# Layer 0 for four pairs at a time, and the first adapter's matrix ahead of it, in a two-layer conditional kernel

## The reference

```
x1[b]  = x[b]  + einsum('ct,cd->dt', x[b], w[subject[b]]) + bias[subject[b]][:, None]
H      = x1[b] @ W.T
xa     = x1[b] @ A[adapter[b]].T                    # rank 16
out[b] = x1[b] + H + (xa @ Bm[adapter[b]].T) * scal[adapter[b]]
```

## Time and profile before

| what | value |
|---|---|
| median of three runs | 266.66 us |
| the profiled execution | 265.84 us |
| its span in the profile | 264.2 us |
| PE busy | 241.5 us, 91% |
| DVE, ACT, POOL busy | 145.2, 113.4, 82.2 us |
| DMA | 36.69 MB, mean 139 GB/s |

### The profile page before, as it was taken

How to read it: one execution, slowest core, us unless ns; L and a number is a source line. 1 busy time by engine, 2 the same in 40 slices (tenths; PEclk the granted TensorE clock), 3 DMA queues, 4 the chain that set the end, 5 groups by cost and what they waited for, 6 DMA issues and landing times.

```text
span 264.2 us, 9940 instructions
## 1 busy us (share of the span) xinstructions
PE 241.5 (91%) x2929; PEld 194.7 (74%) x2930; DVE 145.2 (55%) x244; ACT 113.4 (43%) x189; POOL 82.2 (31%) x284
## 2 busy tenths in 40 slices
PE   0463999899999999999999999999999999999993
PEld 0442888688788888888888887888878887887882
DVE  5657557755565666755575655566675554433200
ACT  2154345544454445444464444544544443333411
POOL 6332342533324333332343332432333333320000
PEclk9977699999999999999999999999999999999999
DMA  6663144555545554655455545555564445552231
GB/s 114 152 186 105 43 133 134 160 139 148 154 144 156 157 159 139 180 154 144 121 177 155 141 140 146 157 152 159 139 188 149 144 127 179 155 156 79 70 78 42
DMA packets 25826, 36.69 MB, mean 139 GB/s; under 512 B 6736, under 2 KB 8784, under 8 KB 25808
## 3 DMA queue, kind: packets, MB, share of 16 engines
q1 hardware_dynamic: 20400, 28.06, 37.2%
q10 hardware_dynamic: 5408, 8.40, 12.3%
HBM read 19.67 MB, written 16.78 MB: 138 GB/s over the span
## 4 chain that ended last, share of the span: by engine, by line
PE 86%; DVE 5%; DMA 3%; issue 2%; ACT 1%; SPq 1%; ACTq 0%; DVEq 0%
PE ps L717 69%; PE ps L702 13%; PE ps L682 2%; DMA x_ring<-in_x_dram 2%; PE ps L664 2%; DVE m_lo L487 1%; DMA ids_i<-in_itok_B_dram 1%; DVE m_f L481 1%; ACT m_hi L563 1%; DVE x L494 0%; ACT x_hi L569 0%; DVE place L453 0%; DVE prec_n L388 0%; PE ps L654 0%; DVE x_lo L502 0%
## 5 line engine op out<-in xcount | busy, mean ns | idle before, releaser
L717 PE MATMUL ps<-m_hi,x_hi 128*128 x264 | 106.9, 405 | 0.8 <-DVE m_lo L487 0.8
L717 PE MATMUL ps<-m_lo,x_hi 128*128 x264 | 103.5, 392 | 0.0
L717 PE MATMUL ps<-m_hi,x_lo 128*128 x264 | 103.4, 392 | 0.0
L502 DVE TENSOR_TENSOR x_lo<-x,x_hi 128x512 fp32r<-128x512 f32 x64 | 44.5, 695 | 86.5 <-ACT x_hi L569 86.5
L359 POOL COPY p_pair<-p_all 64x64 f32 x128 | 45.6, 356 | 135.0 <-DVE x L494 62.0
L578 ACT ACTIVATE o_ring<-ps 128x512 f32<-128x512 f32 x60 | 35.8, 597 | 63.2 <-PE ps L717 62.9
L717 PEld LDWEIGHTS ps<-m_hi,x_hi 128*128 128x128 f32 x264 | 49.9, 189 | 12.6 <-issue 1.6
L717 PEld LDWEIGHTS ps<-m_hi,x_lo 128*128 128x128 f32 x264 | 49.8, 189 | 10.8
L569 ACT ACTIVATE x_hi<-x 128x512 fp32r<-128x512 f32 x64 | 40.4, 632 | 39.8 <-ACT o_ring L578 18.6
L717 PEld LDWEIGHTS ps<-m_lo,x_hi 128*128 128x128 f32 x264 | 49.9, 189 | 9.5
L702 PEld LDWEIGHTS ps<-p_pair,x_ring 64*64 64x64 f32 x2048 | 34.2, 139 | 18.2 <-issue 16.5
(11 more groups left out here) (81 smaller groups left out, 55.5 us busy)
## 6 DMA issues: line engine op xcount, KB each, us to landing
x_ring<-in_x_dram SPq DMA_DIRECT2D x128, 128.0 KB, 2.6
out_dram<-o_ring ACTq DMA_DIRECT2D x64, 128.0 KB, 2.4
out_dram<-o_ring SPq DMA_DIRECT2D x64, 128.0 KB, 2.5
o_ring<-in_L_cond_W_dram SPq DMA_DIRECT2D x4, 256.0 KB, 4.6
a_f<-in_L_cond_A_dram SPq DMA_DIRECT2D x8, 128.0 KB
b_nat<-in_L_cond_Bm_dram SPq DMA_DIRECT2D x1, 256.0 KB, 4.1
p_all<-in_L_cond_weights_dram SPq DMA_DIRECT2D x2, 128.0 KB, 4.3
bias_all<-in_fside_8xS_dram SPq DMA_DIRECT2D x1, 256.0 KB, 5.7
```

The costliest lines, as they stand in the source:

```text
L502: nc.vector.tensor_tensor(x1_lo[:, u % HELD], x1[:, u % 2], x1_hi[:, u % HELD], ALU.subtract).then_inc(x1_lo_ready, 1)
L717: mm = nc.tensor.matmul(ps[:, bank, :], part[:, u % HELD, c, :], m[:, ds(k * (TC * T) + c * T, T)], start=(c == 0 and part is x1_hi and m ...
```

## The change

- Layer 0 is done for four pairs at once, at steps u = 2 and u = 6 alone, for pairs j + 2, j + 4, j + 3, j + 5 in this order; steps u = 0 and u = 4 do none. Step 0 does pairs 2 and 3 as before.
- Two pairs share two banks: an even pair in banks 0 and 1, an odd one in 6 and 7, in columns 0 to 255 or 256 to 511 by u // 2 % 2. The waits on l0_done are counted in the new order, and DVE reads a bank only when both of its pairs are there.
- x is asked for seven pairs ahead instead of six; the ring of x still has four slots.
- The rings p_pair and bias_pair have eight slots instead of four, with POOL's wait counted accordingly.
- Ahead of step 0, PE does the last chunk of W and all four tiles of the first M, and then layer 0 of pairs 0 and 1. DVE and ACT are reordered to match.

```diff
-    AHEAD = 6
+    PR = 8
+    AHEAD = 7
+    L0_QUAD = 4
...
+        def l0_count(j, u):
+            if isinstance(j, int) and j < L0_QUAD:
+                return j + 1
+            return j - u % L0_QUAD + (2, 4)[u % 2]
+
+        def l0_out(u):
+            cols = TC * C * (u // 2 % 2)
+            return ps[:, 6 * (u % 2):6 * (u % 2) + 2, cols:cols + TC * C]
...
             def load_x(j, slot, b):
-                at_least(sp, l0_done, j - XR + 1)
+                at_least(sp, l0_done, j - XR + 1 if isinstance(j, int) and j < XR + L0_QUAD
+                         else j - XR - slot + (1, 3, 2, 4)[slot])
...
-                slot = u % XR
-                at_least(pool, x1_ready, j - XR + 1)
+                slot = u % PR
+                at_least(pool, x1_ready, j - (PR - 1 if n is None else min(PR - 1, HEAD - 1 + (u - HEAD) % BODY)))
...
             def x1_add(j, u):
-                dve.wait_ge(l0_done, j + 1)
+                dve.wait_ge(l0_done, l0_count(j, u))
...
             m_split(0, 0)
+            m_split(1, 1)
+            m_add(2, 2)
+            m_add(3, 3)
             x1_add(0, 0)
-            m_add(2, 2)
+            m_split(2, 2)
             x1_split(0, 0)
-            m_split(1, 1)
-            m_add(3, 3)
-            m_split(2, 2)
+            x1_add(1, 1)
             m_split(3, 3)
-            x1_add(1, 1)
             x1_split(1, 1)
...
-                at_least(pe, x1_ready, j - 1)
+                at_least(pe, x1_ready, j - 1 if isinstance(j, int) and j < L0_QUAD else j - u % L0_QUAD)
...
+            def l0_at(j, u):
+                if isinstance(j, int) and j == 0:
+                    return range(2, L0_QUAD)
+                if u % L0_QUAD == 2 and (not isinstance(j, int) or j + 2 < PAIRS):
+                    return (2, 4, 3, 5)
+                return ()
...
             turn_w(2)
-            layer0_inputs(0, 0)
-            layer0(0, 0)
             turn_w(3)
             m_product(2, 2)
             m_product(3, 3)
             pe.wait_ge(others_ready, 2)
+            layer0_inputs(0, 0)
+            layer0(0, 0)
             layer0_inputs(1, 1)
             layer0(1, 1)
...
             def step(j, u, n):
-                if u % 2 == 0 and (not isinstance(j, int) or j + 2 < PAIRS):
-                    layer0_inputs(j + 2, u + 2)
-                    layer0_inputs(j + 3, u + 3)
+                l0_pairs = l0_at(j, u)
+                for i in l0_pairs:
+                    layer0_inputs(j + i, u + i)
```

More of the change, by code:

```diff
@@ L79, in cond_residual_layers @@
         bias_all = sb("bias_all", [P, S, C])
-        p_pair = sb("p_pair", [P, XR, C])
-        bias_pair = sb("bias_pair", [P, XR, P])
+        p_pair = sb("p_pair", [P, PR, C])
+        bias_pair = sb("bias_pair", [P, PR, P])
         x1 = sb("x1", [P, 2, TC, P])
@@ L489, in x1_add @@
             def x1_add(j, u):
-                dve.wait_ge(l0_done, j + 1)
+                dve.wait_ge(l0_done, l0_count(j, u))
                 at_least(dve, x1_lo_ready, j - 1)
-                bank = l0_banks(u)
                 nc.vector.tensor_tensor(x1[:, u % 2].rearrange("p c (h d) -> p c h d", h=2),
-                                        ps[:, bank:bank + 2, 0:TC * C].rearrange("p h (c d) -> p c h d", c=TC),
-                                        bias_pair[:, u % XR, :].rearrange("p (h d) -> p h d", h=2).unsqueeze(1)
+                                        l0_out(u).rearrange("p h (c d) -> p c h d", c=TC),
+                                        bias_pair[:, u % PR, :].rearrange("p (h d) -> p h d", h=2).unsqueeze(1)
                                         .to_broadcast([P, TC, 2, C]), ALU.add).then_inc(x1_ready, 1)
@@ L618, in _ @@
             act.wait_ge(warmed, 1)
+            m_round(2, 2)
             x1_round(0, 0)
-            m_round(2, 2)
             m_round(3, 3)
@@ L689, in layer0_inputs @@
                 pe.wait_ge(pair_ready, j * 4 + 4)
-                at_least(pe, x1_ready, j - 1)
+                at_least(pe, x1_ready, j - 1 if isinstance(j, int) and j < L0_QUAD else j - u % L0_QUAD)
             def layer0(j, u):
                 slot = u % XR
-                bank = l0_banks(u)
+                x1_t = l0_out(u)
                 for c in range(TC):
@@ L701, in layer0 @@
                             at = c * P + side * C
-                            mm = nc.tensor.matmul(ps[side * C:side * C + C, bank + half, c * C:c * C + C],
-                                                  x_ring[rows, slot, at:at + C], p_pair[rows, slot, :],
+                            mm = nc.tensor.matmul(x1_t[side * C:side * C + C, half, c * C:c * C + C],
+                                                  x_ring[rows, slot, at:at + C], p_pair[rows, u % PR, :],
                                                   start=True, stop=True)
                 mm.then_inc(l0_done, 1)
+            def l0_at(j, u):
[4 more added lines that the diff above has]
+                return ()
             def layer1(j, u, k, bank, done=l1_done, tiles_awaited=False):
@@ L741, in step @@
                 mixed = n_of_mixed(j) is not None
-                if u % 2 == 0 and (not isinstance(j, int) or j + 2 < PAIRS):
-                    layer0_inputs(j + 2, u + 2)
-                    layer0_inputs(j + 3, u + 3)
+                l0_pairs = l0_at(j, u)
+                for i in l0_pairs:
+                    layer0_inputs(j + i, u + i)
                 k = words(pe, regs[:2 if mixed else 1], table[0:1, ds(j * 8 + W_PLACE, 2 if mixed else 1)], K - 1)
-                if u % 2 == 0 and (not isinstance(j, int) or j + 2 < PAIRS):
-                    layer0(j + 2, u + 2)
-                    layer0(j + 3, u + 3)
+                for i in l0_pairs:
+                    layer0(j + i, u + i)
                 if makes_parts(j, u, n) is not None:
```

2 lines of the change are left out of this document (removed).

## The result

The changed kernel takes 277.51 us (median of 4 runs, 276.61 to 278.77) where the kernel before took 266.50 us beside it (4 runs). The ratio is 1.0415, with a 95% interval of 1.0354 to 1.0477: slower, as predicted (278.0 us). The profiled execution took 277.9 us, its span 276.2 us, against 264.2 before. The lines have moved: L711 is layer 0, L734 layer 1, L691 a tile of M, L673 turn_b, L491 m_add, L497 m_split, L503 x1_add, L511 x1_split, L263 the load of x, L256 that of A, L290 SP's store.

What follows compares the result with a forecast made beforehand. PE was taken as the bound (busy 91%, 86% of the chain), other engines as cover. Start 0.1, rounds 9.7 and end 1.65 sum to 11.5; on 265.84 that gives 277.3, with the median 0.82 higher 278.1, said as 278.0; range 269.5 to 281.5.

Steps and rivals of the forecast that it cites:

- batch of four, start to layer 1: PE in the loop: a batch of 128 layer 0 instructions lasts 2.20 us, its second half adding 1.10.
- m_lo holds step 5, restart from the tile: Layer 1 of step 5: PE waits for m_lo and restarts 0.13 us behind it, 4.44 us from the tile of u = 3.
- from there to the batch at u = 2: Loop, u = 6 to u = 2: late x starts the batch at 14.1 us instead of 13.8; price 0.35.
- five rounds: Loop, u = 6 to u = 6: each round +1.95 us, five rounds +9.7.
- end: Last round up to u = 2 (+1.25) and the steps behind it: together +1.65 us.
- start: Ahead of and up to step 2: 2.4 us won but lost waiting for POOL's pair 7; net +0.1 us.
- The batch gone at u = 4: Between tile and layer 1 of step 5: m_lo's chain stays unchanged, so of 1.10 us taken out only 0.2 comes back.
- x at u = 6: Batch at u = 6: SP's late x, behind A, starts it 8.55 us from the tile of u = 3; price 0.7 a round.
- x at u = 2: Batch at u = 2: last x, asked for behind the store of step 7, comes late; price 0.35 us, bounds 0 and 1.0.
- x in time: Rival: x doesn't delay the batch at u = 6, only the m_lo wait remains; +3.4 us, 270.0; chance 0.12.
- PE stays fed: Rival: all 15 changes of kind go (3.0 us) and the start's 2.4 arrive; 261.3 us; chance 0.05.
- The clock: Rival: waits at u = 6 drop the granted clock, 1.7 us lost in each of six rounds; +10, 288; chance 0.06.

Runs made afterwards that it cites:

- q_both: Changed kernel with A asked for at u = 1 instead of u = 3 and the last tile made at u = 2 instead of u = 3: 268.43 us.
- q_a_early: Changed kernel with SP asking for the next adapter's A at u = 1 instead of u = 3: 272.01 us, ratio 1.0184.
- after: The changed kernel itself, with batches of four, against the kernel before: 277.51 us, ratio 1.0415.
- q_grouped: Changed kernel with A at u = 1, last tile at u = 2, b_dup behind pair u = 7, four x requests in a row ahead of stores: 264.54 us.
- p_new_start: Kernel before (batches of two) with only the new order ahead of step 0 on PE, DVE and ACT: 264.42 us, ratio 0.9917.
- q_old_start: Changed kernel with the old order of the start on PE, DVE and ACT: 280.32 us, ratio 1.0478.
- q_tile_early: Changed kernel with the last tile of the next M made at u = 2 instead of u = 3, and its split one step earlier: 285.09 us.
- q8: Changed kernel with x asked for eight pairs ahead instead of seven: 294.96 us, ratio 1.1129.
- q8_both: Changed kernel with A at u = 1, last tile at u = 2, and x asked for eight pairs ahead: 279.87 us, ratio 1.0535.
- q_fed: As q_grouped, but in the loop POOL's own queue loads A behind b_dup, leaving SP x and stores: 265.43 us, ratio 0.9943.

## Why the prediction was right

| step | predicted | measured |
|---|---|---|
| batch of four, start to layer 1 | 2.20 us | 2.02 |
| m_lo holds step 5, restart from the tile | 4.44 | 4.61 |
| batch at u = 6, from the tile | 8.55 | 8.55 to 9.39, mean 8.93 |
| from there to the batch at u = 2 | 14.1 | 14.77 once, then 13.90 to 14.06 |
| five rounds | +9.7 | +10.93 |
| end | +1.65 | +0.66 |
| start | +0.1 | +0.41 |
| sum | +11.5 | +12.0 (276.2 - 264.2) |

Five rounds are the batches at 51.66 and 205.16, 153.50 us, against 142.57 before (51.25 to 193.82).

The waits came where I had put them, and their causes were right in the main. That the sum is out by only 0.5 us is in part luck: the rounds came out 1.2 us dearer and the start 0.3, the end 1.0 cheaper. The 1.2 are 1.9 more for later batches at u = 6, 0.8 more for the first round's wait at u = 2 and 0.3 of small differences, less 1.8 for batches that were cheaper.

*The batch gone at u = 4.* Right. The chain behind the tile didn't change (m_lo at 4.27 to 4.34 us in all five rounds behind the first), and PE waits where I said. q_both against q_a_early shows that this wait is real and its own: taking it away is worth 3.6 us (272.01 to 268.43) once A is out of the way; with A where it was, the same edit cost 7.6 us (277.51 to 285.09). PE restarted 0.33 us behind m_lo, not 0.13, and why is open. Before, layer 1 of step 5 began 4.66 us from its tile in these rounds with PE busy, 0.35 behind m_lo; in after it began 4.61 to 4.68 from it. Measured by that lag, the 0.3 us of cover that I read was none, and of the batch taken out there nothing to 0.05 us came back, not 0.2.

*x at u = 6.* Right in its place and its cause for three rounds of five; q_a_early took 5.5 us away with nothing but SP's order. In the other two I missed a limit. In the fourth round (and the fifth is like it) DVE waits for A:

```profile
170.53 0.74 DVE L476 SCALAR_TENSOR_TENSOR a_parts<-a_parts,neg,a_f 64x512 fp32r<-64x512 f32 x1 [1.33 <-ACT a_parts L561]
171.19 0.73 DVE L482 SCALAR_TENSOR_TENSOR b_parts<-b_parts,neg,ps 128x512 fp32r<-128x512 f32 x1
171.85 0.68 DVE L503 TENSOR_TENSOR x<-ps,bias_pair 128x512 f32<-128x512 f32 x1
```

```profile
169.46 1.15 SPq L263 DMA_DIRECT2D x_ring<-in_x_dram  x2
```

```profile
174.16 1.05 PE L711 MATMUL ps<-p_pair,x_ring 64*64 64x64 f32 x57 [1.40 <-issue]
```

By x the batch could begin at 169.46 + 0.67 + 2.6 + 0.72 = 173.45. It began at 174.16, 1.63 us behind x1_add. The five rounds stood at 8.72, 8.55, 8.74, 9.23 and 9.39 us from the tile: my price was 0.38 a round too small, 1.9 in five, and 1.5 of it lies in these two.

*x at u = 2.* Its size was right (0.35, against 0.25 to 0.41 of idle time, and 1.12 in the first round), its cause only half. In after, x and x1_add allow the batch at about the same moment: at 126.93 x1_add had ended 1.66 us before, and the last x had landed 0.78 us before. q_grouped takes the late x away, and 0.26 us stay (at 91.94 and 178.49). The profile names POOL's copies, but the one that it names ends 0.16 to 0.28 us before the batch, nearer than the 0.72 of a wait with its register load: that copy is for a later pair.

*The batch itself* is 0.18 us cheaper than two batches of two: 64 more instructions take 2.02 - 1.10 = 0.92 us, not 1.10. The 1.10 of a batch of two already holds part of the change of kind: the first 64 instructions of a batch of four last 0.95 us, and from there to layer 1 are 1.07. This is the mis-sized term that hid the missed one: two such batches a round are 0.36 x 5 = 1.8 us, against the 1.9 of the step before. It is also most of the end, where four more such batches (0.7 us) and smaller waits make 0.66 out of 1.65.

*The start.* Every step came 0.3 us later than said: x1_add at 22.81 (22.5), the batch at 23.60 (23.3), pair 7 at 33.97 (33.7), the batch at step 2 at 34.67 (34.4). The gain doesn't arrive because of POOL, as said: the batch at step 2 begins 0.70 us behind the copies for pair 7, and p_new_start and q_old_start bound the gain from both sides. I had read the clock wrong: the earlier trace rows show 3.40 us at half clock, but the stretch before lasted the same 6.8 us (24.0 to 30.8) as after (22.5 to 29.3), with PE busy 5.11 us of it before and 5.70 after.

*The rivals.* "x in time" is nearly q_a_early: 270.0 predicted, 272.01 measured; the batches at u = 2 still waited there, 1.28 us once and 0.25 to 0.34 in the other rounds, which that rival had left out. "PE stays fed" would be 261.3; the nearest thing built, q_grouped, reached 264.5, so it was dearer to reach than that m_lo alone. The clock did not fall in the loop of after, though it did in q_tile_early, q8 and q8_both.

The floor of about 600 ns that the Trainium skill puts under a register load ("DMA: Bandwidth & Descriptors", section "Latency and other measured facts") agrees with the 0.72 us of the earlier trace rows only where the load follows the wait directly. With six instructions of the queue between, the runs show 1.62 to 1.66 at the least.

## What to carry to other kernels

Merging work into larger batches saves a fixed cost per batch, but it gathers all inputs at one point: price the last one to come, and price the queue's own instructions between a wait and the work (some 0.15 us each here, an estimate). By these distances the wait for the latest input belongs last, which no run here tried. When a stretch of work is taken out between a producer and its consumer, look at what it covered; here, moving the last tile by one step and A by two took back 9.1 of the 11.0 us, but the tile alone made it worse by 7.6. And a wait that the profile calls "issue", or puts down to an engine that was done long ago, is to be found by measuring the least distance from each candidate to the work, over all its instances and kernels.

## What the runs showed of the hardware

- The granted clock fell to 0.50 for 3.4 to 6.9 us in three rounds of q_tile_early, beside two waits of PE with one tile between: 1.02 and 1.70 us, 1.49 and 1.66, 0.38 and 1.72. With 0.41 and 1.69, and with 1.03 and 1.70, it stayed at 1.00. In after, 1.01 to 1.08 and then 0.69 to 1.48 us with a layer 1 between left it at 1.00.
- Back to back, SP needs about 2.6 us for a step of two loads and one store, with a register load among them (2.63 in q8's rows), and 7.2 us for eight loads with theirs, 0.9 each (q_fed). An engine that only asks for transfers can be 74% full (2.63 of 3.56 us).
- A batch of 64 small matmuls took 1.10 us from its start to the layer 1 behind it, one of 128 took 2.02: 0.92 us for 64 more, 14 ns each.
- From the end of a wait's cause to the batch behind it: 0.72 us where only the register load follows the wait, 1.62 to 1.66 at the least where six more instructions of the queue stand between.
